# A two-layer graph network with a mixture of experts behind it: one-hots made at other times and in other pieces, bias products with all 128 rows

## The chip, the cores and the metric

The kernel runs on one NeuronCore of a Trainium2 chip. The metric is the time of one execution on the device in microseconds (us), as the median of several runs. The engines are TensorE (PE in the profile; its weight loads, which overlap its matmuls, are PEld), VectorE (DVE), ScalarE (ACT), GpSimd (POOL) and SyncE (SP), which only issues DMAs here.

## The reference

```python
x = x + gnn(layernorm(x))          # x: 6250 nodes x 256, float32
x = x + ffn(layernorm(x))

def rgcn_conv(x, src, dst, edge_type, basis, comp, root, bias):   # R = 8 relations, 4 bases
    W = einsum('rb,bde->rde', comp, basis)
    h = einsum('nd,rde->nre', x, W)
    msg = h[src, edge_type]                      # 206250 edges, sorted by dst
    seg = dst * 8 + edge_type
    mean = segment_sum(msg, seg) / maximum(count(seg), 1)
    return mean.reshape(n, 8, -1).sum(1) + x @ root + bias

h = relu(rgcn_conv(x, ..., layer 0))
h = relu(rgcn_conv(h, ..., layer 1))
gnn = take(einsum('nd,tde->nte', h, lin_w), node_type) + lin_b[node_type]   # 5 node types

# ffn: 8 experts, top 2, D = 256, H = 512
logits = xn @ Wr + br
w = softmax of the top 2 logits, spread over the 8 experts
y = sum over e of w[:, e] * (gelu(xn @ W1[e] + b1[e]) @ W2[e] + b2[e])
```

## The kernel before, in words

Nodes are taken in pairs of blocks: a block is 64 nodes, a pair 128, and there are 49 pairs. The edges are sorted by destination, so a block's edges lie in one window, cut in 18 tiles of 128 edges. For each tile GpSimd gathers 128 rows of the node table (each row three bf16 parts of 256 features) with one indirect DMA (L558) into one of 18 slots. The last tile's gather is issued only where it holds edges. A tile's edges hit at most 64 of the block's 512 (node, relation) columns. VectorE makes a one-hot of 128 x 64 for every tile, all 18 of a block in one instruction (L929): the column numbers `iota_b` compared with each edge's `rel`. TensorE multiplies the gathered rows by the one-hot into PSUM (L1251, six matmuls a tile; in layer 0 a seventh, L1247, counts the edges).

When a block's 18 tiles are summed, VectorE scales the sums by 1/count into `scaled` (`scale`, L945). In layer 0 it first makes `inv` from the counts (L938, L939); in layer 1 `inv` comes back from memory. For a pair, `mix_bases` (L911 for the first relation, L913 for the other seven) mixes the eight relations into four bases, and TensorE's `transform` (L1283) multiplies them by the bases. `h` is 0 for the even block of a pair and 1 for the odd one; `hot`, `idx`, `rel` and `inv` are double over it.

Who waits for whom: a gather waits for its slot to be free (`used[k]`, raised by TensorE every third tile); a tile's matmuls wait for the gather; a block's first tile waits for its one-hots (`hot_ready`) and for VectorE to have scaled the block before it (`sc_ready`), since both sum into the same banks; `one_hots` waits for the tables that SP loads (`idx_in`) and for the block that used the same half of `hot`. SP works through one list: the even block's tables, the even block's `inv`, behind the odd block's scale, the odd block's tables, its `inv`, the node data.

Layer 0's loop (`first_layer` on VectorE) goes, for pair p: scale the even block, one-hots of the next even block, scale the odd block, `save`, mix, one-hots of the next odd block. Layer 1's loop (`second_layer`; `dense` on TensorE and ScalarE) does three pairs at once: block work of one pair, the type-wise product and layer norm of the pair before it (`typed`, `margin`, `route`), and the eight experts of the pair before that. The order is written out by hand: on VectorE, one-hots of the next even block, root and masks, experts 0 and 1, `typed`, expert 2, scale the odd block, mix, `margin`, mix, expert 3, `route`, then mixing and experts 4, 5 and 6 in turn, one-hots of the next odd block, scale the even block, expert 7. `plain` is a memset of one column that holds a wait ahead of a branch.

Three products bring a bias in with few rows: the types' bias (L1314, `tmaskT` of 5 rows times `linb_sb`), the experts' second bias (L1410, `wfT` of 8 rows times `b2_sb`), and the router's bias (L1329, one row of ones times `br_sb`). The last is added to the logits in PSUM (L1328 gives the logits), and VectorE copies them out (L997).

Of the kernel before, what the change touches and what calls it, by code (L numbers as in the profile page):

```python
# [68 lines left out]
def build(nc, x, src, dst, etype, ntype, basis0, comp0, root0, bias0, basis1, comp1, root1, bias1,  # L69
          lin_w, lin_b, gamma, beta, Wr, br, W1, b1, W2, b2, out):  # L70
    with ExitStack() as ctx:
# [37 lines left out]
        linb_sb = sb("linb_sb", [TYPES, D], F32)  # L109
        b2_sb = sb("b2_sb", [EXPERTS, D], F32)  # L110
        br_sb = sb("br_sb", [1, EXPERTS], F32)
# [18 lines left out]
        tmaskT = sb("tmaskT", [TYPES, P], F32)  # L130
# [15 lines left out]
        wfT = sb("wfT", [EXPERTS, P], F32)  # L146
# [191 lines left out]
        def _(sp):  # L338
# [41 lines left out]
            sp.dma_start(linb_sb[:, :], lin_b).then_inc(weights_in, 16)  # L380
            sp.dma_start(b2_sb[:, :], b2).then_inc(weights_in, 16)
            sp.dma_start(br_sb[:, :], br.rearrange("(a e) -> a e", a=1)).then_inc(weights_in, 16)
# [139 lines left out]
        def _(gp):  # L522
# [17 lines left out]
            gp.iota(pid[:, :], [[0, 1]], base=0, channel_multiplier=1, allow_small_or_imprecise_dtypes=True)  # L540
            gp.memset(ident[:, :], 0.0).then_inc(s_const, 1)
# [77 lines left out]
        def _(act_):  # L619
# [79 lines left out]
            def dense(a=None, r=None, n=P):  # L699
                if r is not None:  # L700
                    gelu(r, 0)
                    gelu(r, 1)
                if a is not None:
                    relu(1, a + PAIRS, a)
                if r is not None:
                    gelu(r, 2)
                if a is not None:
                    deviation(a, 0)
                    deviation(a, 1)
                if r is not None:  # L710
                    gelu(r, 3)
                if a is not None:
                    act_.wait_ge(znT_done, START + a + 1)
                    if not isinstance(a, int) or a > 0:
                        act_.wait_ge(lg_done, a)
                    for k in range(HALVES):
                        last = sc.activation(xnext[:, k, :], T2[:, k * P:(k + 1) * P], ACT.Identity,
                                             bias=beta_sb[:, k:k + 1], scale=gamma_sb[:, k:k + 1])
                    last.then_inc(xnext_done, 1)
                if r is not None:  # L720
                    gelu(r, 4)
                if a is not None:
                    act_.wait_ge(margin_done, a + 1)
                    sc.activation(soft[:, 1:2], soft[:, 0:1], ACT.Tanh, scale=0.5).then_inc(tanh_done, 1)
                if r is not None:
                    gelu(r, 5)
                    gelu(r, 6)
                    act_.wait_ge(wfT_ps, r + 1)
                    sc.activation(wfT[:, :], T2[0:EXPERTS, 256:256 + P], ACT.Copy).then_inc(wfT_done, 1)
                    gelu(r, 7)  # L730
                if a is not None:
                    act_.wait_ge(xnext_done, a + 1)
                    sc.activation(xnT[:, :, :], xnext[:, :, :], ACT.Copy).then_inc(xnT_done, 1)
                if r is not None:
                    act_.wait_ge(y_acc, 2 * START + (r + 1) * EXPERTS)
                    act_.dma_start(out[bass.ds(r * P, n), :], o[0:n, :]).then_inc(out_done, 16)
# [9 lines left out]
        def _(dve):  # L746
# [173 lines left out]
            def one_hots(h, G):  # L920
                with dve.If(general):
                    pass
                with dve.Else():
                    one_hots_fast(h, G)

            def one_hots_fast(h, G):
                dve.wait_ge(idx_in[h], G * 48 + 48)
                summed(dve, G, h, back=2)
                v.tensor_tensor(hot[:, h, :, :], iota_b[:, :].unsqueeze(1).broadcast_to([P, TILES, COLS]),  # L929
                                rel[:, h, :].unsqueeze(2).broadcast_to([P, TILES, COLS]),  # L930
                                ALU.is_equal).then_inc(hot_ready, 1)
# [44 lines left out]
            def masks(p):  # L976
                dve.wait_ge(node_in, p * 48 + 48)
                v.tensor_scalar(tmask[:, :], iota8[:, 0:TYPES], ntcol[:, 0:1], None, ALU.is_equal)
                v.tensor_scalar(tmaskT[:, :], ntrow[:, :], pid[0:TYPES, 0:1], None,
# [15 lines left out]
            def margin(p):  # L995
                dve.wait_ge(lg_done, p + 1)
                v.tensor_copy(lg[:, :], LG).then_inc(lg_read, 1)  # L997
# [34 lines left out]
            def first_layer():  # L1032
                one_hots(0, 0)
                one_hots(1, 0)
                for h in range(2):
                    scale(0, h, 0, 0)
                    if h == 0:
                        one_hots(0, 1)
                mix_bases(0, 0)
                one_hots(1, 1)  # L1040
                base = ch.base + ch.n

                def body(p, more=True):
                    scale(0, 0, p, p)
                    if more:
                        one_hots(0, p + 1)
# [3 lines left out]
                    if more:  # L1050
                        one_hots(1, p + 1)
# [10 lines left out]
            def second_layer():  # L1062

                def body(a=None, r=None, y=None, x=None):
                    if x is not None:
                        plain(1)
                        one_hots(0, x + PAIRS)
# [21 lines left out]
                    for e, (first, last_) in ((4, (8, 16)), (5, (16, 24)), (6, (24, MIXES))):  # L1089
                        if y is not None:  # L1090
                            mix_bases(1, y + PAIRS, first, last_)
                        if r is not None:
                            expert(r, e)
                    if x is not None:
                        plain(3)
                        one_hots(1, x + PAIRS)
# [7 lines left out]
                one_hots(0, PAIRS)  # L1104
                plain(3)
                one_hots(1, PAIRS)
# [25 lines left out]
        def _(pe):  # L1132
# [190 lines left out]
            def logits(q):  # L1323
# [3 lines left out]
                for k in range(HALVES):  # L1327
                    t.matmul(LG, xnext[:, k, :], wr_sb[:, k, :], start=(k == 0), stop=False)  # L1328
                t.matmul(LG, ones_f[0:1, :], br_sb[:, :], start=False, stop=True).then_inc(lg_done, 1)  # L1329
# [156 lines left out]
```

## Time and profile before

| | |
|---|---|
| median of 3 runs | 4807.63 us (4806.77 to 4810.96) |
| the profiled execution's own time | 4807.05 us |
| its span | 4805.2 us |
| PE busy | 3782.7 us, 79% |
| PEld busy | 3282.0 us, 68% |
| DVE busy | 3014.4 us, 63% |
| ACT busy | 880.3 us, 18% |
| POOL busy | 3332.3 us, 69% |

Busy time is the time in which an engine had an instruction of its own running; waits, branches and the issuing of a DMA by SP or ACT are not in it. Matmuls are pipelined, so a busy PE is not a PE at its peak. Some 200 us of setting up (layer norm, tables) come first, then layer 0 to about 2350 us, then layer 1, and the last pairs' experts from 4700 us on. The shares of the whole span mix these stages.

### The profile page before, as it was taken

The page shows a single profiled execution, that of the slowest core. Times are in us where ns is not written, and L with a number is a line of the kernel's source. Part 1 is how long each engine was busy: PE and PEld are TensorE (multiplying, and loading weights), DVE is VectorE, ACT ScalarE, POOL GpSimd, SP SyncE. Part 2 cuts the span into 40 slices and gives each one's busy share as a digit, 9 for nine tenths or more (in the row PEclk, how much of TensorE's full clock was granted, in tenths as well). Part 3 has the DMA queues.
Part 4 walks back from the last instruction along what each step waited for, and adds up shares of the span by engine and source line. Part 5 has one row for each costly group of instructions (what it writes and reads, how often), then busy time and mean ns, then how long its engine had stood idle before and what let it go on. Part 6 is the DMA issues. An engine that isn't in the chain of part 4 may idle for free.

```text
span 4805.2 us, 119647 instructions
## 1 busy us (share of the span) xinstructions
PE 3782.7 (79%) x38119; PEld 3282.0 (68%) x38120; DVE 3014.4 (63%) x6579; ACT 880.3 (18%) x2470; POOL 3332.3 (69%) x3374
## 2 busy tenths in 40 slices
PE   1366666666666666666559999999999999999999
PEld 1255555555555555555448888888888888888888
DVE  4556656766666676666446676767666666666663
ACT  2200000000000000000003333333333333333333
POOL 0477777777777777777477777777777777676770
PEclk9555555555555555555569999999999999999999
DMA  4656655555555555555456555555555555555550
GB/s 128 194 172 183 176 158 156 158 158 157 156 158 158 155 159 157 156 157 159 115 168 168 160 160 160 157 161 156 160 159 162 157 160 161 157 161 157 162 160 21
DMA packets 344661, 749.10 MB, mean 156 GB/s; under 512 B 128323, under 2 KB 167806, under 8 KB 344430
## 3 DMA queue, kind: packets, MB, share of 16 engines
q0 software_dynamic: 215040, 662.09, 49.0%
q1 hardware_dynamic: 115510, 70.49, 5.6%
q10 hardware_dynamic: 14076, 16.04, 1.0%
q8 instruction: 23, 0.38, 0.0%
q14 instruction: 12, 0.10, 0.0%
HBM read 719.00 MB, written 29.35 MB: 156 GB/s over the span
## 4 chain that ended last, share of the span: by engine, by line
PE 43%; DVE 24%; issue 15%; DMA 9%; POOL 8%; DVEq 1%; SPq 0%; ACT 0%; POOLq 0%; ACTq 0%
DVE mixed L913 11%; POOL slot L558 8%; PE bank L1251 8%; PE bank L1338 8%; PE bank L1283 8%; PE bank L1351 8%; DMA slot<-table,idx 7%; DVE inv L939 4%; PE bank L1247 3%; DVE scaled L945 3%; PE bank L1311 2%; PE bank L1312 2%; DVE o L1024 2%; PE bank L1279 1%; DVE inv L938 1%
## 5 line engine op out<-in xcount | busy, mean ns | idle before, releaser
L558 POOL DMA_INDIRECT slot<-table,idx x3354 | 3326.6, 992 | 1308.2 <-issue 1045.0
L1251 PE MATMUL bank<-hot,slot 128*128 (+1 forms) x21168 | 1240.9, 211 | 63.2 <-DMA slot<-table,idx 54.6
L1251 PEld LDWEIGHTS bank<-hot,slot 128*128 128x128 bf16 x21168 | 994.4, 108 | 125.6 <-issue 69.2
L1247 PE MATMUL bank<-hot,ones_b 128*128 x1764 | 398.7, 226 | 744.9 <-DMA slot<-table,idx 337.8
L1247 PEld LDWEIGHTS bank<-hot,ones_b 128*128 128x128 bf16 x1764 | 180.9, 103 | 1007.1 <-issue 969.3
L1338 PE MATMUL bank<-xnT,ffn_w 128*128 128x128 f32 x6272 | 791.4, 279 | 49.2 <-DVE scaled L945 49.1
L1338 PEld LDWEIGHTS bank<-xnT,ffn_w 128*128 128x128 f32 x6272 | 740.7, 192 | 80.7 <-DVE scaled L945 58.3
L1351 PE MATMUL bank<-ffn_w,act 128*128 128x256 f32 x3136 | 761.6, 386 | 0.3 <-DVE o L1024 0.2
L1351 PEld LDWEIGHTS bank<-ffn_w,act 128*128 128x128 f32 x3136 | 565.5, 190 | 78.0 <-issue 16.9
L913 DVE SCALAR_TENSOR_TENSOR mixed<-scaled,small,mixed 128x256 f32<-128x256 f32 x1372 | 573.7, 481 | 12.2
L913 DVE SCALAR_TENSOR_TENSOR mixed<-scaled,comp_sb,mixed 128x256 f32<-128x256 f32 x1372 | 573.5, 481 | 10.5
L938 DVE TENSOR_SCALAR inv<-bank 128x512 f32<-128x512 f32 x98 | 67.5, 689 | 777.3 <-PE bank L1251 777.3
L691 ACT ACTIVATE act<-bank,small 128x128 f32<-128x128 f32 x1568 | 441.7, 373 | 542.6 <-PE bank L1338 541.5
L1283 PE MATMUL bank<-mixed,basis_sb 128*128 128x128 f32 x3136 | 472.2, 310 | 0.0
L1283 PEld LDWEIGHTS bank<-mixed,basis_sb 128*128 128x128 f32 x3136 | 451.7, 227 | 0.0
L945 DVE TENSOR_TENSOR scaled<-bank,inv 128x512 f32<-128x512 f32 x392 | 377.0, 1039 | 62.2 <-PE bank L1251 48.7
L939 DVE RECIPROCAL inv<-inv 128x512 f32<-128x512 f32 x98 | 328.6, 3353 | 3.4
L1024 DVE SCALAR_TENSOR_TENSOR o<-bank,wfull,o 128x256 f32<-128x256 f32 x343 | 164.9, 481 | 252.6 <-PE bank L1351 247.5
L929 DVE TENSOR_TENSOR hot<-iota_b,rel 128x1152 bf16<-128x1152 bf16 x196 | 265.0, 1353 | 44.4 <-issue 29.7
L665 ACT ACTIVATE hcur<-bank,small 128x128 f32<-128x128 f32 x98 | 30.6, 363 | 1118.0 <-PE bank L1283 1027.2
L691 ACT ACT_TABLE_LOAD x96 | 123.2, 1283 | 374.3 <-DVE o L1024 373.4
L988 DVE SCALAR_TENSOR_TENSOR x<-bank,tmask,x 128x256 f32<-128x256 f32 x196 | 94.9, 484 | 116.3 <-PE bank L1312 116.3
(148 smaller groups left out, 2189.0 us busy)
## 6 DMA issues: line engine op xcount, KB each, us to landing
slot<-table,idx POOLq DMA_INDIRECT x3354
inv<-inv_d SPq DMA_DIRECT2D x98, 256.0 KB, 3.7
table<-ffn_w SPq DMA_DIRECT2D x7, 1344.0 KB, 6.0
table<-parts ACTq DMA_DIRECT2D x49, 192.0 KB, 3.2
ffn_w<-in_L_ffn_W_dram SPq DMA_DIRECT2D x16, 512.0 KB
xcur<-in_x_dram SPq DMA_DIRECT2D x48, 128.0 KB
out_dram<-o ACTq DMA_DIRECT2D x48, 128.0 KB
ffn_w<-in_x_dram SPq DMA_DIRECT2D x6, 896.0 KB, 8.9
```

Of the source, the lines that this page charges most:

```text
L558: gp.indirect_dma_start(out=slot[:, k, :], out_offset=None, in_=table[layer], in_offset=bass.IndirectOffsetOnAxis(ap=idx[:, h, k:k + 1], a ...
L691: last = sc.activation(act[:, e % 2, c, :], HP[e % 2][:, c * P:(c + 1) * P], ACT.Gelu, bias=b1_sb[:, e * HCH + c:e * HCH + c + 1])
L913: ins = v.scalar_tensor_tensor(out=mixed[:, b, :, :], in0=scaled[:, :, r, :], scalar=s, in1=mixed[:, b, :, :], op0=ALU.mult, op1=ALU.add)
L929: v.tensor_tensor(hot[:, h, :, :], iota_b[:, :].unsqueeze(1).broadcast_to([P, TILES, COLS]), rel[:, h, :].unsqueeze(2).broadcast_to([P, TI ...
L939: ch.link(v.reciprocal(iv, iv))
L945: last = v.tensor_tensor(scaled[:, k, :, h * BD:(h + 1) * BD].rearrange("p r n -> p n r"), S[k][:, :].rearrange("p (n r) -> p n r", r=R), ...
L1024: v.scalar_tensor_tensor(out=o[:, :], in0=YP[e % 2][:, 0:D], scalar=wfull[:, 0, e:e + 1], in1=acc[:, :], op0=ALU.mult, op1=ALU.add).then_i ...
L1247: t.matmul(C[:, at], ones_b[:, :], oh, start=(k == 0), stop=(k == TILES - 1), skip_group_check=True)
L1251: last = t.matmul(S[f][:, at], slot[:, k, q * D + f * P:q * D + (f + 1) * P], oh, start=(k == 0 and q == 0), stop=(k == TILES - 1 and q == ...
L1283: last = t.matmul(T[:, o_ * P:(o_ + 1) * P], basis_sb[:, b, k, o_ * P:(o_ + 1) * P], mixed[:, b, k, :], start=(layer == 1 and n == 1), sto ...
L1338: last = t.matmul(HP[e % 2][:, c * P:(c + 1) * P], w1_sb[:, e, k, c * P:(c + 1) * P], xnT[:, k, :], start=(k == 0), stop=(k == HALVES - 1))
L1351: last = t.matmul(YP[e % 2][:, 0:D], act[:, e % 2, c, :], w2_sb[:, e, c, :], start=(c == 0), stop=(c == HCH - 1))
```

## The change

1. In layer 1, the one-hots of the next odd block are made behind expert 5, and no longer behind expert 6 and its bias sum.
2. In layer 0, the one-hots of a block are made in 18 instructions of one tile each (a tensor_scalar with `rel` as a scalar per row), and no longer in one tensor_tensor. Layer 1 keeps the one instruction.
3. `tmaskT`, `wfT`, `linb_sb` and `b2_sb` get 128 rows. GpSimd sets them to zero at the start; the masks, weights and biases fill the first 5 or 8 rows, and the two products run over 128 rows. SP waits for GpSimd's third constant before it loads the biases.
4. The router's bias is loaded to all 128 rows and added by VectorE as it takes the logits out of PSUM; TensorE's product for it goes.

```diff
-        linb_sb = sb("linb_sb", [TYPES, D], F32)
-        b2_sb = sb("b2_sb", [EXPERTS, D], F32)
-        br_sb = sb("br_sb", [1, EXPERTS], F32)
+        linb_sb = sb("linb_sb", [P, D], F32)
+        b2_sb = sb("b2_sb", [P, D], F32)
+        br_sb = sb("br_sb", [P, EXPERTS], F32)
...
-        tmaskT = sb("tmaskT", [TYPES, P], F32)
+        tmaskT = sb("tmaskT", [P, P], F32)
...
-        wfT = sb("wfT", [EXPERTS, P], F32)
+        wfT = sb("wfT", [P, P], F32)
...
-            sp.dma_start(linb_sb[:, :], lin_b).then_inc(weights_in, 16)
-            sp.dma_start(b2_sb[:, :], b2).then_inc(weights_in, 16)
-            sp.dma_start(br_sb[:, :], br.rearrange("(a e) -> a e", a=1)).then_inc(weights_in, 16)
+            sp.wait_ge(s_const, 3)
+            sp.dma_start(linb_sb[0:TYPES, :], lin_b).then_inc(weights_in, 16)
+            sp.dma_start(b2_sb[0:EXPERTS, :], b2).then_inc(weights_in, 16)
+            sp.dma_start(br_sb[:, :], br.partition_broadcast(P)).then_inc(weights_in, 16)
...
+            for z in (linb_sb, b2_sb, tmaskT, wfT):
+                gp.memset(z[:, :], 0.0)
...
-                    sc.activation(wfT[:, :], T2[0:EXPERTS, 256:256 + P], ACT.Copy).then_inc(wfT_done, 1)
+                    sc.activation(wfT[0:EXPERTS, :], T2[0:EXPERTS, 256:256 + P], ACT.Copy).then_inc(wfT_done, 1)
...
-            def one_hots_fast(h, G):
-                dve.wait_ge(idx_in[h], G * 48 + 48)
-                summed(dve, G, h, back=2)
-                v.tensor_tensor(hot[:, h, :, :], iota_b[:, :].unsqueeze(1).broadcast_to([P, TILES, COLS]),
-                                rel[:, h, :].unsqueeze(2).broadcast_to([P, TILES, COLS]),
-                                ALU.is_equal).then_inc(hot_ready, 1)
+                    dve.wait_ge(idx_in[h], G * 48 + 48)
+                    summed(dve, G, h, back=2)
+                    if layer == 0:
+                        for k in range(TILES):
+                            last = v.tensor_scalar(hot[:, h, k, :], iota_b[:, :], rel[:, h, k:k + 1], None,
+                                                   ALU.is_equal)
+                    else:
+                        last = v.tensor_tensor(hot[:, h, :, :],
+                                               iota_b[:, :].unsqueeze(1).broadcast_to([P, TILES, COLS]),
+                                               rel[:, h, :].unsqueeze(2).broadcast_to([P, TILES, COLS]),
+                                               ALU.is_equal)
+                    last.then_inc(hot_ready, 1)
...
-                v.tensor_scalar(tmaskT[:, :], ntrow[:, :], pid[0:TYPES, 0:1], None,
+                v.tensor_scalar(tmaskT[0:TYPES, :], ntrow[:, :], pid[0:TYPES, 0:1], None,
                                 ALU.is_equal).then_inc(mask_done, 1)
...
-                v.tensor_copy(lg[:, :], LG).then_inc(lg_read, 1)
+                v.tensor_tensor(lg[:, :], LG, br_sb[:, :], ALU.add).then_inc(lg_read, 1)
...
+                        if e == 5 and x is not None:
+                            plain(3)
+                            one_hots(1, 1, x + PAIRS)
                     if x is not None:
-                        plain(3)
-                        one_hots(1, x + PAIRS)
                         scale(1, 0, x + PAIRS, x)
...
-                    t.matmul(LG, xnext[:, k, :], wr_sb[:, k, :], start=(k == 0), stop=False)
-                t.matmul(LG, ones_f[0:1, :], br_sb[:, :], start=False, stop=True).then_inc(lg_done, 1)
+                    last = t.matmul(LG, xnext[:, k, :], wr_sb[:, k, :], start=(k == 0), stop=(k == HALVES - 1))
+                last.then_inc(lg_done, 1)
```

## Rows read from the trace of the kernel before

**Rows 1.** Stretches: busy us (x instructions) of PE, PEld, DVE, ACT, POOL; clock, DMA.

```profile
300.00:2260.00 1960.00, 1309.24 (x13372) 1055.21 (x13371) 1241.97 (x1980) 62.64 (x176) 1498.72 (x1515) 0.58 0.57 160
2360.00:4700.00 2340.00, 2209.64 (x22533) 2005.18 (x22534) 1506.28 (x4025) 721.20 (x2048) 1664.71 (x1677) 0.97 0.57 159
```

**Rows 2.** Line L558 from 300 to 2260 us: ns minimum/median/maximum, first and last start.

```profile
L558 POOL DMA_INDIRECT slot<-table,idx x1515: 942/946/1865, 299.4 to 2259.9; - x190
```

**Rows 3.** GpSimd in order of time, layer 0: start, us, instruction, idle before it.

```profile
1041.11 1.36 POOL L558 DMA_INDIRECT slot<-table,idx  x1 [0.30 <-issue]
...
1047.77 1.83 POOL L558 DMA_INDIRECT slot<-table,idx  x1 [0.31 <-issue]
...
1071.14 1.01 POOL L558 DMA_INDIRECT slot<-table,idx  x1 [0.30 <-issue]
```

**Rows 4.** VectorE in order of time, a pair of layer 0.

```profile
1040.30 1.35 DVE L929 TENSOR_TENSOR hot<-iota_b,rel 128x1152 bf16<-128x1152 bf16 x1
1041.57 0.69 DVE L938 TENSOR_SCALAR inv<-bank 128x512 f32<-128x512 f32 x1
...
1047.45 1.34 DVE L929 TENSOR_TENSOR hot<-iota_b,rel 128x1152 bf16<-128x1152 bf16 x1
1063.84 0.69 DVE L938 TENSOR_SCALAR inv<-bank 128x512 f32<-128x512 f32 x1 [15.05 <-PE bank L1251]
...
1071.25 1.27 DVE L911 TENSOR_SCALAR mixed<-scaled,small 128x256 f32<-128x256 f32 x4
...
1085.66 0.69 DVE L938 TENSOR_SCALAR inv<-bank 128x512 f32<-128x512 f32 x1
```

**Rows 5.** TensorE's matmuls in order of time: tiles 0 and 11 of an odd block, layer 0.

```profile
1047.95 0.20 PE L1247 MATMUL bank<-hot,ones_b 128*128 x1 [0.82 <-DVE scaled L945]
...
1055.79 0.23 PE L1247 MATMUL bank<-hot,ones_b 128*128 x1
```

**Rows 6.** VectorE in order of time, a period of layer 1.

```profile
3057.54 0.17 DVE L997 COPY lg<-bank 128x8 f32<-128x8 f32 x1 [0.55 <-PE bank L1329]
...
3073.06 0.42 DVE L1029 TENSOR_TENSOR o<-o,bank 128x256 f32<-128x256 f32 x1
...
3073.93 1.36 DVE L929 TENSOR_TENSOR hot<-iota_b,rel 128x1152 bf16<-128x1152 bf16 x1 [0.33 <-issue]
3075.21 1.90 DVE L945 TENSOR_TENSOR scaled<-bank,inv 128x512 f32<-128x512 f32 x2
...
3083.90 0.22 DVE L978 TENSOR_SCALAR tmask<-iota,ntcol 128x5 f32<-128x5 f32 x1
3084.03 0.47 DVE L979 TENSOR_SCALAR tmaskT<-ntrow,pid 5x128 f32<-5x128 int32 x1
...
3101.23 1.96 DVE L945 TENSOR_TENSOR scaled<-bank,inv 128x512 f32<-128x512 f32 x2 [0.22 <-DVE o L1024]
...
3104.98 0.17 DVE L997 COPY lg<-bank 128x8 f32<-128x8 f32 x1 [0.40 <-PE bank L1329]
```

**Rows 7.** TensorE's matmuls in order of time, the same period.

```profile
3077.16 2.05 PE L1338 MATMUL bank<-xnT,ffn_w 128*128 128x128 f32 x16 [1.07 <-DVE scaled L945]
...
3094.52 0.59 PE L1311 MATMUL bank<-linw_sb,hcur 128*128 128x256 f32 x2
3094.95 0.59 PE L1312 MATMUL bank<-linw_sb,hcur 128*128 128x256 f32 x2
...
3096.10 2.05 PE L1338 MATMUL bank<-xnT,ffn_w 128*128 128x128 f32 x16
...
3104.05 0.51 PE L1328 MATMUL bank<-wr_sb,xnext 128*128 128x8 f32 x4
3104.49 0.38 PE L1329 MATMUL bank<-br_sb,ones_f 1*128 1x8 f32 x2
```

**Rows 8.** GpSimd in order of time, layer 1: its one long wait in a period.

```profile
3060.76 0.94 POOL L558 DMA_INDIRECT slot<-table,idx  x1 [3.47 <-PE bank L1251]
```

More of the change, by code:

```diff
@@ L918, in mix_bases, with one_hots @@
                     ins.then_inc(mixed_ready, 1)
-            def one_hots(h, G):
+            def one_hots(layer, h, G):
                 with dve.If(general):
@@ L923, in one_hots @@
                 with dve.Else():
-                    one_hots_fast(h, G)
-            def one_hots_fast(h, G):
-                dve.wait_ge(idx_in[h], G * 48 + 48)
-                summed(dve, G, h, back=2)
-                v.tensor_tensor(hot[:, h, :, :], iota_b[:, :].unsqueeze(1).broadcast_to([P, TILES, COLS]),
-                                rel[:, h, :].unsqueeze(2).broadcast_to([P, TILES, COLS]),
-                                ALU.is_equal).then_inc(hot_ready, 1)
+                    dve.wait_ge(idx_in[h], G * 48 + 48)
[10 more added lines that the diff above has]
+                    last.then_inc(hot_ready, 1)
             def scale(layer, h, G, p):
@@ L1032, in first_layer @@
             def first_layer():
-                one_hots(0, 0)
-                one_hots(1, 0)
+                one_hots(0, 0, 0)
+                one_hots(0, 1, 0)
                 for h in range(2):
@@ L1037, in first_layer @@
                     if h == 0:
-                        one_hots(0, 1)
+                        one_hots(0, 0, 1)
                 mix_bases(0, 0)
-                one_hots(1, 1)
+                one_hots(0, 1, 1)
                 base = ch.base + ch.n
@@ L1045, in body @@
                     if more:
-                        one_hots(0, p + 1)
+                        one_hots(0, 0, p + 1)
                     scale(0, 1, p, p)
@@ L1050, in body @@
                     if more:
-                        one_hots(1, p + 1)
+                        one_hots(0, 1, p + 1)
                 per = 4 + (R - 1)
@@ L1066, in body @@
                         plain(1)
-                        one_hots(0, x + PAIRS)
+                        one_hots(1, 0, x + PAIRS)
                     if a is not None:
@@ L1103, in second_layer @@
                 plain(1)
-                one_hots(0, PAIRS)
+                one_hots(1, 0, PAIRS)
                 plain(3)
-                one_hots(1, PAIRS)
+                one_hots(1, 1, PAIRS)
                 scale(1, 0, PAIRS, 0)
```

## The prediction, made before the changed kernel was run

> **What bounds the kernel now.** I read first the table of stretches [rows 1]: a piece of layer 0's loop, then layer 1's loop. In layer 0 no engine looks full: GpSimd is busy 1498.72 of 1960 us, VectorE 1242, TensorE 1309 at a granted clock of 0.58. In layer 1 TensorE is busy 2209.64 of 2340 us at 0.97. Two stages, two limits.
>
> For layer 0 the next view is GpSimd's one line, the gathers [rows 2]: 1515 in 1960 us, median 946 ns, mean 1498.72/1515 = 989 ns, each with 0.30 us of issue ahead of it [rows 3]. 1498.7 + 1515 x 0.30 = 1953 us: the stretch is filled by gathers and their gaps, and layer 0 lasts as long as its gathers. Mean over median is 43 ns x 1515 = 65 us in 1960, or 1.5 us of each pair of blocks; a pair takes 1085.66 - 1041.57 = 44.09 us [rows 4]. What makes some of them long is seen by holding GpSimd's order of time [rows 3] against VectorE's [rows 4]. The gather at 1041.11 took 1.36 us instead of 0.95; the one-hots of a whole block (L929) ran from 1040.30 to 1041.65. The gather at 1047.77 took 1.83; the other one-hots ran from 1047.45 to 1048.79. Both gathers ended some 0.8 us after the one-hots: a gather that begins inside that instruction stands until it is over, and then takes what it has left. That is 0.41 + 0.88 = 1.3 us of each pair, nearly all of the 1.5.
>
> For layer 1 I read both engines in order of time [rows 6, 7]. The period is 3104.98 - 3057.54 = 47.44 us, in two halves. From the logits' copy (3057.54) to the end of the even block's `scaled` (3077.11), 19.6 us, VectorE goes through margin, mixing, experts 3 to 6, one-hots and scale and is late: TensorE stood 1.07 us before 3077.16 for it. From there to the end of the logits (3104.87), 27.7 us, TensorE sets the time. What TensorE saves in its half counts; what it saves in VectorE's half doesn't.
>
> **Layer 0's one-hots, tile by tile.** Removed per pair: two instructions of 1.27 us (1040.30 to 1041.57 [rows 4]), and with them 1.3 us of GpSimd's time. Added: 36 compares of 64 columns with one scalar per row. The trace has none of that size; the nearest rows bound it. `tmask` (L978), 5 columns and a scalar per row, is followed by L979 after 0.13 us [rows 6]: the lower bound. L911, 256 columns, takes 1.27 us for four, the last 0.35 at most, so (1.27 - 0.35)/3 = 0.31 each [rows 4]: the upper bound. 64 columns are a quarter of the way, so I take 0.13 + 0.18/4 = 0.175 us. A set of 18 is 3.15 us (bounds 2.3 and 5.6), 1.9 more than now.
>
> What does such a train do to a gather? The nearest row is the gather at 1071.14, which meets L911's four from 1071.25 on and takes 1.01 us: 0.06 over [rows 3, 4]. It doesn't stand until a train is over, but for a part of one instruction. A set of 3.15 us meets 2.5 gathers (one each 1.25 us), two sets 5: 0.3 us a pair (bounds nothing, and 0.13 each, a whole compare: 0.65). GpSimd saves 1.3 - 0.3 = 1.0 us a pair; in 47 pairs **-47 us**, if GpSimd stays the limit.
>
> Does it? The ring behind it: odd block's `inv` over mixing and odd one-hots to the even block's `inv` (1063.84 to 1085.66, 21.8 us); that `inv` to TensorE's first tile of the odd block (1041.57 to 1047.95, 6.4); its 18 tiles at TensorE's own pace (1047.95 to 1055.79 for 11, 0.71 each, 12.8) [rows 4, 5]. That is 41.0 us against 44.1, so TensorE still catches up with the gathers. The longer set lies in this ring: 42.9 against 44.1 - 1.0 = 43.1. The cover is used up to 0.2 us. The even one-hots (1047.45) lie before 15 us of VectorE's idle time and cost nothing.
>
> The Trainium skill (SBUF — State Buffer, "Who interferes with whom") says that VectorE and GpSimd share a port pair as an exclusive lock, and that a tensor_scalar in a two-port mode takes it; the gathers that end right behind L929 agree with blocking, and L911's row shows only 0.06 us of it. The Trainium skill (VectorE: DVE Perf Modes, "The TRN2 errata") speaks against many small tiles: 58 + FD/Accel cycles each, an estimate of 77 ns a compare, 1.4 us a set; no row is that fast.
>
> **Router's bias.** TensorE's two L1329 go, so `lg` can start when L1328 ends, 3104.05 + 0.51 = 3104.56, not 3104.87 [rows 7]: **-0.31 us**, at the seam of the halves. The add in place of the 0.17 us copy has one input more; I take 0 and bound it at 0.02.
>
> **128 rows for the bias products.** L1312 starts 0.43 us after L1311 (3094.52 to 3094.95), two matmuls of 256 columns. L1338 could then start 0.86 us after L1312, with the 5-row L1314 between; it starts at 3096.10, 1.15 after it [rows 7]. So a visit to 5 rows costs 0.29 us; **-0.29** in TensorE's half. Below it may be nothing (given back by the layer norm's chain on VectorE and ScalarE), above 0.4. L1410 (8 rows) lies in VectorE's half: nothing. The Trainium skill (TensorE: Matmul & The Clock Gate, "LDWEIGHTS") has a load of 32 rows take as long as one of 128; by that alone padding would bring nothing, and the gap in the row speaks against it.
>
> **Odd one-hots two experts ahead.** They stay in VectorE's unbroken half, so their 1.27 us and the 0.45 in front of them (3073.48 to 3073.93, memset and branch) are paid earlier, not saved. What is hidden changes: `scaled` at 3075.21 started before the one-hots had ended, its semaphore checks covered. Directly behind an expert's sum it starts 0.22 us late (3101.23) [rows 6], and here there is one check more. **+0.25 us** a period; bounds 0 and 0.35. Queued behind them are mixing's last quarter, expert 6 and the b2 sum, 1.7 us later; only the next transform, 6 us on, needs those. SP loads their `rel` behind the odd `scaled` of 3101.23, some 14 us before they want it. A gather may stand 0.9 us for them, but GpSimd waits 3.47 us for used slots each period [rows 8].
>
> Layer 1: -0.31 - 0.29 + 0.25 = -0.35 us, x 48 = **-17 us**. The four memsets and SP's wait on them lie at the start, where VectorE waits for the edges: 0. The last two bodies have no blocks: about -1.
>
> **Sum.** The profiled execution took 4807.05 us (span 4805.2), the median is 4807.63, 0.6 above. 4807.6 - 47 - 17 - 1 = 4742.6; I say **4742**.
>
> **Rivals.** (a) VectorE's ring takes over in layer 0. For it: 0.2 us of cover. It begins at 43.1 - 41.0 = 2.1 us more a set, 0.187 us a compare. At 0.22 the ring is 43.7, layer 0 gives 0.4 x 47 = 19, the time is 4771; at 0.31 the ring is 45.3, 1.2 us longer than a pair now, and it is 4846. Against it: four times fewer columns than L911. Chance 0.17, 0.03 of it beyond 0.24.
> (b) A set holds GpSimd out to its end, as one instruction does now. It decides from the first gather that starts in a set: it would stand 3.15 us less its offset, some 2.4 on average, twice a pair, instead of 1.3: +3.5 us, x 47 = +164, 4953. Against it: the gather of 1.01 us at L911's four. It needs compares that follow each other without a gap for GpSimd. Chance 0.05. A lock as the Trainium skill has it ends with each instruction.
> (c) The padded rows bring nothing: 4742 + 14 = 4756. Chance 0.10.
> (d) The moved one-hots cost nothing: 4742 - 12 = 4730. Chance 0.15.
> The forecast itself: 0.53.
>
> **Numbers.** The range goes from all of 1.3 us saved together with (d), 4742 - 14 - 12 = 4716, to the middle of (a) with (c), 4785; outside are (b) and the far end of (a). This kernel's measurement tells about 0.2% (9.6 us) from no change. Faster 0.90, same 0.03 (between the two ends of (a)), slower 0.07.
>
> **What would show it.** After: layer 0's pair at 43.1 us; no gather of 1.36 or 1.83 beside the one-hots; sets of 2.3 to 3.3 us; GpSimd's gap still 0.30 at every gather. Layer 1: a period of 47.1 us, L1338 0.43 behind the bias product, `scaled` 0.2 to 0.35 behind the b2 sum. Wrong would be: gathers that wait for TensorE's L1251 in layer 0 (a), or gathers of 2 us and more (b).

## The result, and the profile after

| | before | after |
|---|---|---|
| median, us | 4807.2 (4804.32 to 4810.96, 4 runs) | 4725.92 (4724.51 to 4728.75, 4 runs) |
| the profiled execution's own time | 4807.05 | 4726.16 |
| its span | 4805.2 | 4724.1 |

The ratio is 0.9831, with a 95% interval of 0.9814 to 0.9848: 81 us less, where 65 were forecast.

Where the 81 us come from is read off the first and last gather of each layer. The view is the gathers' source line, over the whole of layer 0 and the whole of layer 1: ns minimum/median/maximum, then first and last start. First the kernel before:

```profile
L558 POOL DMA_INDIRECT slot<-table,idx x1677: 942/946/2149, 173.2 to 2344.7; - x187
...
L558 POOL DMA_INDIRECT slot<-table,idx x1677: 940/946/1898, 2389.9 to 4694.2; - x187
```

And the changed kernel:

```profile
L561 POOL DMA_INDIRECT slot<-table,idx x1677: 942/946/1152, 173.2 to 2282.3; - x187
...
L561 POOL DMA_INDIRECT slot<-table,idx x1677: 940/946/1978, 2326.7 to 4615.8; - x187
```

Both reach the first gather at 173.2 us. Layer 0's gathers take 2109.1 us instead of 2171.5 (-62.4), the step between the layers 44.4 instead of 45.2 (-0.8), layer 1's gathers 2289.1 instead of 2304.3 (-15.2), and what follows the last gather 4724.1 - 4615.8 = 108.3 instead of 111.0 (-2.7). Forecast were -47, 0, -17 and -1. The longest gather of layer 0 fell from 2149 to 1152 ns, while layer 1 still has its long ones.

Layer 0's stretch of the changed kernel, as in [rows 1]:

```profile
300.00:2260.00 1960.00, 1357.56 (x13754) 1089.45 (x13754) 1411.20 (x3585) 64.87 (x182) 1485.43 (x1559) 0.58 0.58 165
```

In the same 1960 us of layer 0 there are 1559 gathers instead of 1515, in less busy time: 1485.43/1559 = 953 ns on average instead of 989. 1485.4 + 1559 x 0.30 = 1953 us: gathers and their gaps fill the stretch as before. GpSimd is still the limit, and the granted clock is the same 0.58. None of the 1576 gathers that start between 300 us and the layer's end has more than 0.35 us of idle time ahead of it, so none waited for TensorE.

VectorE in order of time, a pair of layer 0, beside [rows 4]:

```profile
1036.61 0.69 DVE L945 TENSOR_SCALAR inv<-bank 128x512 f32<-128x512 f32 x1 [10.96 <-PE bank L1259]
...
1045.33 11.92 DVE L916 SCALAR_TENSOR_TENSOR mixed<-scaled,small,mixed 128x256 f32<-128x256 f32 x28
1057.17 3.03 DVE L931 TENSOR_SCALAR hot<-iota_b,rel 128x64 bf16<-128x64 bf16 x18
1059.87 0.68 DVE L945 TENSOR_SCALAR inv<-bank 128x512 f32<-128x512 f32 x1
...
1065.74 2.77 DVE L931 TENSOR_SCALAR hot<-iota_b,rel 128x64 bf16<-128x64 bf16 x18
1079.33 0.69 DVE L945 TENSOR_SCALAR inv<-bank 128x512 f32<-128x512 f32 x1 [10.82 <-PE bank L1259]
```

The pair is 1079.33 - 1036.61 = 42.72 us here, 42.79 as the median of all. A set takes 1059.87 - 1057.17 = 2.70 us, 0.15 a compare. GpSimd beside it, as in [rows 3]:

```profile
1049.05 1.01 POOL L561 DMA_INDIRECT slot<-table,idx  x1 [0.30 <-issue]
...
1057.99 0.95 POOL L561 DMA_INDIRECT slot<-table,idx  x1 [0.30 <-issue]
1059.24 0.96 POOL L561 DMA_INDIRECT slot<-table,idx  x1 [0.30 <-issue]
...
1066.75 0.95 POOL L561 DMA_INDIRECT slot<-table,idx  x1 [0.30 <-issue]
1068.00 0.95 POOL L561 DMA_INDIRECT slot<-table,idx  x1 [0.30 <-issue]
```

The four gathers that begin in the two sets take 0.95 and 0.96 us. Over the whole of layer 0 from 300 us on, 182 gathers begin inside a compare and take 950 ns on average, 979 at most: next to nothing. The gathers of 1.01 us lie beside the mixing, which is the same in both kernels.

Layer 1, VectorE in order of time, beside [rows 6]:

```profile
2989.63 0.17 DVE L1004 TENSOR_TENSOR lg<-bank,br_sb 128x8 f32<-128x8 f32 x1 [0.16 <-PE bank L1336]
...
3001.74 1.36 DVE L934 TENSOR_TENSOR hot<-iota_b,rel 128x1152 bf16<-128x1152 bf16 x1 [0.33 <-issue]
...
3006.82 0.42 DVE L1036 TENSOR_TENSOR o<-o,bank 128x256 f32<-128x256 f32 x1
3007.57 1.89 DVE L952 TENSOR_TENSOR scaled<-bank,inv 128x512 f32<-128x512 f32 x2 [0.33 <-DVE o L1036]
```

TensorE in the same period, beside [rows 7]:

```profile
2989.01 0.51 PE L1336 MATMUL bank<-wr_sb,xnext 128*128 128x8 f32 x4
2989.37 2.03 PE L1346 MATMUL bank<-xnT,ffn_w 128*128 128x128 f32 x16
...
3009.52 2.05 PE L1346 MATMUL bank<-xnT,ffn_w 128*128 128x128 f32 x16 [1.75 <-DVE scaled L952]
3011.41 0.69 PE L1259 MATMUL bank<-hot,slot 128*128 128x64 bf16 x18
3011.93 3.82 PE L1291 MATMUL bank<-mixed,basis_sb 128*128 128x128 f32 x32
3015.58 1.89 PE L1359 MATMUL bank<-ffn_w,act 128*128 128x256 f32 x8
...
3027.30 0.59 PE L1320 MATMUL bank<-linw_sb,hcur 128*128 128x256 f32 x2
3027.74 0.65 PE L1322 MATMUL bank<-linb_sb,tmaskT 128*128 128x256 f32 x2
3028.22 1.95 PE L1346 MATMUL bank<-xnT,ffn_w 128*128 128x128 f32 x16
```

The period's median is 47.11 us instead of 47.43. From `lg` to the end of the even `scaled` it is 3009.46 - 2989.63 = 19.83 us (before 3077.11 - 3057.54 = 19.57): +0.26. The rest is 27.28 instead of 27.87: -0.6. TensorE's wait for `scaled` grew from 1.07 to 1.75 us, since TensorE arrives 0.42 us earlier and VectorE 0.26 later: what was saved of TensorE's work in VectorE's half turned into that wait (e4 and e5 below show the parts).

### The profile page after: what moved, and what is told of

The parts are those of the page before. It is cut to its first block, busy times and chain, and to the rows that moved or that the text cites. A ratio compares the mean times of both kernels' runs of the same rounds, so it can differ in the third digit from the quotient of the medians.

```text
span 4724.1 us, 121121 instructions
## 1 busy us (share of the span) xinstructions
PE 3743.5 (79%) x38021; PEld 3276.7 (69%) x38022; DVE 3155.1 (67%) x8245; ACT 880.1 (19%) x2470; POOL 3283.6 (70%) x3378
## 4 chain that ended last, share of the span: by engine, by line
PE 38%; DVE 36%; issue 15%; POOL 5%; DMA 4%; DVEq 1%; ACT 0%; SPq 0%; POOLq 0%; ACTq 0%
DVE mixed L916 17%; PE bank L1259 9%; PE bank L1346 8%; PE bank L1359 8%; DVE inv L946 6%; POOL slot L561 5%; PE bank L1291 4%; PE bank L1255 3%; DVE scaled L952 3%; PE bank L1319 2%; DMA slot<-table,idx 2%; PE bank L1320 2%; DVE hot L931 2%; DVE o L1031 1%; DVE mixed L914 1%
## 5 line engine op out<-in xcount | busy, mean ns | idle before, releaser
L561 POOL DMA_INDIRECT slot<-table,idx x3354 | 3277.0, 977 | 1279.6 <-issue 1043.7
L1259 PE MATMUL bank<-hot,slot 128*128 (+1 forms) x21168 | 1254.9, 213 | 63.1 <-DMA slot<-table,idx 54.3
L1346 PE MATMUL bank<-xnT,ffn_w 128*128 128x128 f32 x6272 | 786.1, 279 | 80.6 <-DVE scaled L952 80.6
L1346 PEld LDWEIGHTS bank<-xnT,ffn_w 128*128 128x128 f32 x6272 | 745.9, 193 | 97.3 <-DVE scaled L952 89.4
L931 DVE TENSOR_SCALAR hot<-iota_b,rel 128x64 bf16<-128x64 bf16 x1764 | 280.7, 260 | 6.4 <-DMA off<-off_d 6.4
```

What stands on the lines that cost most here:

```text
L561: gp.indirect_dma_start(out=slot[:, k, :], out_offset=None, in_=table[layer], in_offset=bass.IndirectOffsetOnAxis(ap=idx[:, h, k:k + 1], a ...
L931: last = v.tensor_scalar(hot[:, h, k, :], iota_b[:, :], rel[:, h, k:k + 1], None, ALU.is_equal)
L1259: last = t.matmul(S[f][:, at], slot[:, k, q * D + f * P:q * D + (f + 1) * P], oh, start=(k == 0 and q == 0), stop=(k == TILES - 1 and q == ...
L1346: last = t.matmul(HP[e % 2][:, c * P:(c + 1) * P], w1_sb[:, e, k, c * P:(c + 1) * P], xnT[:, k, :], start=(k == 0), stop=(k == HALVES - 1))
```

## The experiments

"Pair" is the median distance of the even blocks' `inv` in layer 0, "period" that of `lg` in layer 1. Every time stands beside runs of the kernel before on the same chip. "..." in a diff stands for lines left out. For the first four that kernel took 4811.54 us (15 runs).

**e1, the one-hots by tiles in layer 0, nothing else.**

```diff
...
+                    for k in range(TILES):
+                        last = v.tensor_scalar(hot[:, h, k, :], iota_b[:, :], rel[:, h, k:k + 1], None,
+                                               ALU.is_equal)
+                    last.then_inc(hot_ready, 1)
...
```

> The kernel before with layer 0's one-hots made tile by tile and nothing else. Theory (a gather that begins inside the whole-block one-hots stands until they end; short compares don't hold it): layer 0's pair goes from 44.09 to 42.8 us as in the changed kernel, gathers in layer 0 average 0.95 us, layer 1's period stays 47.43; 4807 - 62 = 4745 us. The sum as forecast (0.06 us for each gather met) would give 4760. Rival (layer 0's gain comes from somewhere else in the change): 4800 to 4807.

Measured: 4748.07 us, ratio 0.9867 (0.9850 to 0.9883), 63.5 us less. Pair 42.85, period 47.43 as before, a gather of layer 0 956 ns on average. So the whole gain of layer 0 is this part's.

**e2, the changed kernel with the odd one-hots back behind expert 6.**

```diff
-                        if e == 5 and x is not None:
-                            plain(3)
-                            one_hots(1, 1, x + PAIRS)
                     if x is not None:
+                        plain(3)
+                        one_hots(1, 1, x + PAIRS)
```

> The changed kernel with the odd one-hots of layer 1 back behind expert 6 and its bias sum. Theory (the move only uncovers the semaphore checks ahead of the even scale, 0.26 us of VectorE's unbroken half): period of layer 1 47.11 - 0.26 = 46.85 us, 4726 - 12 = 4714 us. Rival (being early helps: experts or TensorE wait less): period 47.11 or more, 4726 us or more.

Measured: 4718.31 us, ratio 0.9805 (0.9789 to 0.9822), period 46.85. The changed kernel's period is 0.25 us longer, 48 x 0.25 = 12 us. By the medians it is 7.6 us slower, but the two stood beside different runs of the kernel before; by their ratios (0.9831 and 0.9805) it is 12 us too. The move is a loss.

**e3, the kernel before with that move alone** (the opposite diff).

> The kernel before with only the odd one-hots of layer 1 made behind expert 5. Theory: period of layer 1 47.43 + 0.26 = 47.69 us, 4807 + 12 = 4819 us. Rival (the move is free): 4807; (the move helps) under 4800.

Measured: 4823.36 us, ratio 1.0027 (1.0018 to 1.0037), period 47.71: +0.28. In this kernel the even `scaled` starts behind 0.33 us of idle time, as it does at 3007.57 above.

**e4, 128 rows for the two bias products, nothing else** (the change's third part).

> The kernel before with only the two bias products over 128 rows (zeroed rows, SP's wait). Theory (5 rows cost TensorE 0.29 us more than 128 in its own half of the period, 8 rows cost nothing because TensorE waits there): period 47.43 - 0.30 = 47.13 us, 4807 - 15 = 4792 us. Rival (the number of rows doesn't matter): 47.43, 4807 us. Rival (given back by the layer norm's chain): gaps on TensorE gone, but y of expert 2 found waiting for the norm, 47.4.

Measured: 4796.28 us, ratio 0.9969 (0.9957 to 0.9982), period 47.14: -0.29; pair 44.12. TensorE's wait for `scaled`:

```profile
3077.39 2.05 PE L1341 MATMUL bank<-xnT,ffn_w 128*128 128x128 f32 x16 [1.35 <-DVE scaled L948]
```

It is 1.36 us as the median of the periods instead of 1.07, while VectorE's half, from `lg` to the end of the even `scaled`, stays at 19.55 us. So the 128 rows of the experts' product save TensorE some 0.29 us in VectorE's half, and all of it comes back as waiting; the period's gain is that of the types' product.

**e5, the router's bias by VectorE, nothing else** (the fourth part). Here and for e6 to e8 the kernel before took 4808.18 us (10 runs).

> The kernel before with only the router's bias taken from TensorE and added by VectorE. Theory (the logits' end lies at the seam of the two halves): period of layer 1 47.43 - 0.31 = 47.12 us, 15 us less than the kernel before beside it. Rival (TensorE has slack, VectorE's mixing ends as late): 47.43, the same time.

Measured: 4793.39 us, ratio 0.9970 (0.9958 to 0.9981), period 47.15: -0.28. TensorE's wait for `scaled` is 1.16 us. The parts add up: 47.43 - 0.29 - 0.28 = 46.86, and e2 has 46.85.

**e6, e2 with TensorE's wait for `scaled` put behind the up products of the first two experts, no longer between them.** `open_block` holds the waits for `sc_ready` and `hot_ready`, `ups(e)` are an expert's first products, and `more` runs the block's first three tiles.

```diff
                 ups(0)
+                ups(1)
                 more = open_block(y, 1)
-                ups(1, RUN)
+                more(RUN)
```

> The kernel of e2_no_move with one change on TensorE: in layer 1 the wait for the even block's scale stands behind the up products of expert 1, which don't need it, and no longer ahead of them. Theory (TensorE stands some 1.5 us a period at that wait, 19.6 us of VectorE's half being the longer way): the wait is covered by 1.8 us of matmuls, the period goes from 46.85 to 45.4 us, 70 us less than e2_no_move, 4648 us. Rival (the wait isn't what sets the period; it is slack that comes back as another wait, of GpSimd's gathers above all, 34.2 x 1.25 = 42.8 us and 1.5 of long ones): 46.5 to 46.9 us, less than 20 us gained.

Measured: 4671.92 us, ratio 0.9720 (0.9703 to 0.9736). Period 45.88: 0.97 less than e2's, not the 1.5 expected. TensorE's wait for `scaled`, 1.44 us in e2, is gone, but the block's first tiles suffer. TensorE in order of time:

```profile
2947.18 3.73 PE L1345 MATMUL bank<-xnT,ffn_w 128*128 128x128 f32 x32
2950.75 0.34 PE L1258 MATMUL bank<-hot,slot 128*128 128x64 bf16 x6
2951.30 0.79 PE L1258 MATMUL bank<-hot,slot 128*128 128x64 bf16 x12 [0.22 <-issue]
2952.10 2.13 PE L1290 MATMUL bank<-mixed,basis_sb 128*128 128x128 f32 x17
```

VectorE's `scaled` in the same view:

```profile
2948.63 1.94 DVE L952 TENSOR_TENSOR scaled<-bank,inv 128x512 f32<-128x512 f32 x2
```

Three tiles are 0.52 us elsewhere (3011.41 to 3011.93 in the changed kernel); here they take 2952.10 - 2950.75 = 1.35. `scaled` ends at 2950.57, just before them. My reading: TensorE's sequencer stood at the wait until then, behind the queued products, and only afterwards prepared the tiles' addresses. e12 tests where the wait stands; what the sequencer does is in no view.

**e7, layer 0's one-hots in three instructions of six tiles**, in the old form (on the kernel before).

```diff
...
+                    for k in range(0, TILES, 6):
+                        last = v.tensor_tensor(hot[:, h, k:k + 6, :],
+                                               iota_b[:, :].unsqueeze(1).broadcast_to([P, 6, COLS]),
+                                               rel[:, h, k:k + 6].unsqueeze(2).broadcast_to([P, 6, COLS]),
+                                               ALU.is_equal)
...
```

> The kernel before with layer 0's one-hots in three instructions of six tiles, in the same form (tensor_tensor, two inputs from SBUF) as the one. Theory (a gather that begins inside an instruction of this form stands until that instruction is over, whatever follows): each piece is 0.53 us long, a gather loses at most that and 0.25 on average over those that begin in a set; layer 0's gathers average 0.955 to 0.975 us, the pair 43.0 to 43.5 us, 30 to 50 us less than before. Rival (the form itself is at fault, and a set holds gathers for its whole 1.6 us): gathers over 0.99 us, pair 44.1 or more.

Measured: 4776.95 us, ratio 0.9934 (0.9918 to 0.9951): half of e1's gain. Pair 43.41, gathers 972 ns. The total came as expected, but the rows show something more. The pieces' own line (ns minimum/median/maximum):

```profile
L931 DVE TENSOR_TENSOR hot<-iota_b,rel x270: 523/551/564, 328.7 to 2259.7; 128x384 bf16<-128x384 bf16 x135
```

In order of time, the two sets of a pair, then the two gathers that meet them:

```profile
1069.18 1.49 DVE L931 TENSOR_TENSOR hot<-iota_b,rel 128x384 bf16<-128x384 bf16 x3
1076.48 1.46 DVE L931 TENSOR_TENSOR hot<-iota_b,rel 128x384 bf16<-128x384 bf16 x3
...
1069.99 1.50 POOL L558 DMA_INDIRECT slot<-table,idx  x1 [0.30 <-issue]
...
1076.80 1.04 POOL L558 DMA_INDIRECT slot<-table,idx  x1 [0.30 <-issue]
```

Pieces of 0.55 us start (1.49 - 0.55)/2 = 0.47 apart, so the second set's first piece ends at 1077.03; the gather of 1076.80 ended at 1077.84, 0.81 later, as the gathers of [rows 3] do behind L929. It stood for one piece. The gather of 1069.99 began in the second piece, which ended at 1070.20; it ended at 1071.49, 0.82 after the third piece (1070.67). It stood through two pieces. So cutting the instruction does not always let a gather in between: the next piece can take over. It goes by where in a piece the gather begins. Of the 91 gathers that begin in a piece, the 45 that begin 0.17 to 0.33 us after its start stood for that piece alone; the 45 that begin 0.34 to 0.36 us after the start of a second piece stood for the third as well; one that begins 0.02 us into a set stood through all three (2.28 us).

Is it the instruction's length or its form (two tensors from SBUF instead of one tensor and a scalar per row)? The trace of the kernel before says more on this than the experiment. VectorE, then GpSimd, in layer 0:

```profile
1064.57 3.35 DVE L939 RECIPROCAL inv<-inv 128x512 f32<-128x512 f32 x1
1070.91 0.43 DVE L960 TENSOR_TENSOR parts<-rest,parts 128x256 bf16<-128x256 f32 x1 [0.48 <-ACT parts L674]
...
1064.90 0.94 POOL L558 DMA_INDIRECT slot<-table,idx  x1 [0.30 <-issue]
1066.15 0.94 POOL L558 DMA_INDIRECT slot<-table,idx  x1 [0.30 <-issue]
```

The reciprocal, with one tensor as input, is 3.35 us long and holds neither gather. Of the 1580 gathers of layer 0 from 300 us on, 932 overlap no VectorE instruction with two tensors from SBUF, 326 of them the reciprocal: none takes more than 955 ns. Of the 70.8 us over the median that layer 0's gathers take, 70.5 lie in the other 648. So length alone holds no gather here. One tensor as input is no guarantee either: in layer 1, 49 gathers beside float32 tensor_scalars of 256 columns (L911, L969) take up to 1.08 us. What a whole block's one-hots would do as one instruction with a scalar input was not run.

**e8, e2 with layer 1's odd one-hots by tiles as well.**

```diff
-                    if layer == 0:
+                    if layer == 0 or h == 1:
```

> The kernel of e2_no_move with the odd one-hots of layer 1 tile by tile too. Theory (they lie in VectorE's unbroken half, which is the longer way): a set takes 2.6 us instead of 1.27, the period goes from 46.85 to 48.2 us, 65 us more than e2_no_move. Rival (GpSimd's long gathers matter in layer 1 as in layer 0): the period falls under 46.85.

Measured: 4866.67 us, ratio 1.0125 (1.0102 to 1.0148), period 49.80. The sign is right; the loss against e2, 2.95 us a period and 148 us in all, is more than double what was expected. TensorE in order of time in one period:

```profile
3093.90 3.79 PE L1345 MATMUL bank<-xnT,ffn_w 128*128 128x128 f32 x16 [2.88 <-DVE scaled L952]
3097.48 1.17 PE L1258 MATMUL bank<-hot,slot 128*128 128x64 bf16 x18
3098.46 4.51 PE L1290 MATMUL bank<-mixed,basis_sb 128*128 128x128 f32 x32
3102.80 1.89 PE L1358 MATMUL bank<-ffn_w,act 128*128 128x256 f32 x8
```

The windows ahead of and over these rows (columns as in [rows 1]):

```profile
3076.00:3091.00 15.00, 15.00 (x170) 13.76 (x168) 14.25 (x45) 2.71 (x10) 11.65 (x12) 1.00 0.48 136
3093.90:3102.80 8.90, 8.90 (x66) 8.84 (x67) 1.88 (x4) 3.56 (x9) 6.66 (x6) 0.66 0.59 171
```

The longer set makes TensorE's stand 2.88 us instead of e2's 1.44. Then the same three groups take 3102.80 - 3093.90 = 8.90 us where the changed kernel needs 6.06 (3009.52 to 3015.58): 2.84 more, at a granted clock of 0.66 on average, so that part of them ran at the lower level, 1.2 GHz instead of 2.4. The periods of this run bear it out. The stand is there in each of 46 periods, 2.86 to 3.14 us long, but the clock of the 8.9 us behind it is not the same: 1.00 in 7 of them, with periods of 48.2 to 48.6 us; 0.81 to 0.84 in 20, with 49.5 to 50.1; 0.65 to 0.68 in 19, with 51.0 to 51.3. The first is e2's 46.85 and the 1.43 us of the longer set, which is what was expected; the last is that and the 2.84 us. What decides between the three these runs don't show.

**e9, e10, e11, all three beside a kernel before of 6062.01 us (6029.54 to 6099.13, 15 runs).** e9 is e6 with the opening put behind `transform` as well (the diff below, against e2); e10 is e6's edit on the changed kernel, with the move; e11 is the kernel before with 128 rows for `wfT` and `b2_sb` only.

```diff
                 ups(0)
-                more = open_block(y, 1)
-                ups(1, RUN)
+                ups(1)
                 if a is not None:
                     transform(1, a + PAIRS, a)
+                more = open_block(y, 1)
+                more(RUN)
```

> e6_late_open with the wait one step later still, behind the transform too, and the odd block's first three tiles with it. Theory (in e6_late_open TensorE has no idle time to speak of, but its sequencer stands at the wait until 2950.6 and then loads the block's registers in the open, 1.35 us for three tiles that take 0.52 elsewhere; VectorE's half is still the longer way by a hair): behind the transform the wait is long over, the period goes from 45.88 to 45.1-45.3 us, all of it TensorE's work, 30 us less than e6_late_open, 4640 us. Rival (the tiles' cost is the switch from float32 to bf16 or the gathers' pace, 44.4 us): 45.8 to 45.9.

> The changed kernel, so with the odd one-hots two experts ahead, and e6_late_open's later wait. Theory (VectorE's half still decides when the wait ends, and the move lengthens it by 0.26 us): period 45.88 + 0.26 = 46.14 us. Rival (TensorE is full and VectorE has room): 45.88 us.

> The kernel before with only the experts' bias product over 128 rows. Theory (it lies in VectorE's half, where TensorE waits 1.07 us a period afterwards; all of e4_rows_only's gain is the types' bias): period 47.43 us, and TensorE's wait for the even scale grows from 1.07 to 1.4 us; the same time. Rival (both products pay): period 47.3.

Measured: e9 6149.43 us, ratio 1.0126 (1.0086 to 1.0166), period 64.18, pair 55.21. e10 6116.23, ratio 1.0083 (1.0058 to 1.0109), 63.19 and 55.16. e11 6077.63, ratio 1.0014 (0.9990 to 1.0038), 63.02 and 53.99. On this chip the kernel before is 26% longer, and e9's kernel 33% longer than in e12 below, so none of the three questions was answered here. What differs is seen in e11, TensorE in order of time inside a tile of layer 0, and GpSimd 44 us later:

```profile
1004.43 0.21 PE L1254 MATMUL bank<-hot,slot 128*128 x1 [1.17 <-issue]
1005.15 0.39 PE L1254 MATMUL bank<-hot,slot 128*128 x4 [0.51 <-issue]
...
1047.72 0.95 POOL L561 DMA_INDIRECT slot<-table,idx  x1 [5.95 <-PE bank L1254]
```

TensorE stands 0.5 and 1.2 us between matmuls of one tile, waiting for nothing that the profile shows, and GpSimd waits for TensorE to free slots. The gathers themselves are as ever (993 ns on average in e11, 956 in e9). So GpSimd no longer sets layer 0's time. With the longer sets the pair is 1.2 us longer by the medians (55.2 against 54.0), and layer 0 from first to last gather 30 us longer (2701 and 2700 against 2670), or 0.6 us a pair, instead of 1.3 shorter. That is the sign of rival (a), the ring of VectorE and TensorE, on a chip where TensorE's instructions come late; that the sets cost it there is argued, since no run on that chip has them alone. Why the instructions come late stays open.

**e12, the kernel of e9 once more.** The kernel before took 4809.92 us (4806.15 to 4810.68, 7 runs) beside it.

> The kernel of e9 again: e6 with TensorE's opening of the odd block moved once more, behind the transform of the last tile's neighbour, so that TensorE reaches it only when VectorE has ended scaled. Theory (what e6 still lost, 0.5 us a period, is TensorE's sequencer standing at the wait until scaled ends and only then loading the registers of the block's first tiles): where the kernel before takes about 4808 us beside it, layer 1's period is 45.1 to 45.6 instead of e6's 45.88 and the time 4635 to 4660 us, pair of layer 0 42.8. Rival (TensorE's later opening only moves the same work behind the later tile and makes VectorE's first compare late): the period 45.8 to 46.3 and the time 4670 to 4695. If the kernel before takes about 6060 beside it, as in e9, neither can be told and the ratio is 1.00 to 1.02 again.

Measured: 4640.35 us (4639.93 to 4640.95, 4 runs), ratio 0.9649 (0.9632 to 0.9665), period 45.05, pair 42.83. It beats the kernel before by 170 us and the changed kernel, which ran at another time, by some 86. The period is just under the 45.1 to 45.6 expected. TensorE in order of time around the place:

```profile
2942.14 3.73 PE L1345 MATMUL bank<-xnT,ffn_w 128*128 128x128 f32 x32
2945.71 3.74 PE L1290 MATMUL bank<-mixed,basis_sb 128*128 128x128 f32 x32
2949.28 0.69 PE L1258 MATMUL bank<-hot,slot 128*128 128x64 bf16 x18
2949.80 1.97 PE L1358 MATMUL bank<-ffn_w,act 128*128 128x256 f32 x8
```

There is no idle time left, and the three tiles take 0.52 us again. Against e6 this is 0.84 us a period: exactly what the slow tiles cost there (1.35 - 0.52 = 0.83). So the tiles were slow because of where the wait stood: e9's rival (the switch from float32 to bf16, which is here too) and e12's (the opening only moves) fall. It fits the reading of e6, without showing the sequencer itself.

The numbers also say what a stand costs beside the wait. The same work in e2:

```profile
3053.92 1.95 PE L1345 MATMUL bank<-xnT,ffn_w 128*128 128x128 f32 x16
3057.32 2.05 PE L1345 MATMUL bank<-xnT,ffn_w 128*128 128x128 f32 x16 [1.46 <-DVE scaled L952]
...
3063.39 1.89 PE L1358 MATMUL bank<-ffn_w,act 128*128 128x256 f32 x8
```

From the first L1345 to L1358 TensorE needs 3063.39 - 3053.92 = 9.47 us here and 2949.80 - 2942.14 = 7.66 in e12: 1.81 less, of which the wait is 1.46. So 0.35 us more goes with the stand. That also explains e6, where the slow tiles gave part of it back: 1.81 - 0.83 = 0.98, and 0.97 was measured.

## Why the prediction was right, and where its sizes were off

**What bounds layer 0** was right: after the change, gathers and gaps still fill the stretch, and e1's gain of 63.5 us comes with the gathers' mean alone (956 ns).

**Layer 0's term was too small: -62.4 us, not -47.** Its step was "five gathers met, 0.06 us each: 0.3 us a pair" given back. The term measured is next to nothing: the 182 gathers that begin in a compare take 950 ns on average, so all of the 1.3 us is kept. The price came from a misread row. The gather of 1071.14 begins inside L960, a tensor_tensor that runs from 1070.91 to 1071.34 (shown under e7), and not in L911's train, which starts at 1071.25; so it is no price for scalar compares. In layer 0 of the kernel before, the 55 gathers that begin inside L911 take 949 ns at most (in layer 1 some take more). A smaller part is the count: gathers run over 49 pairs, 62.4/49 = 1.27 us each; I used 47. The lower end of the range already had "all of 1.3 us saved".

**The compare was put at 0.175 us and takes 0.15,** a set 2.70 us instead of 3.15. That weakens rival (a): the cover, put at 0.2 us, is 42.8 - (41.0 + 1.4) = 0.4 us by the same sum, even with the shorter pair. The Trainium skill (VectorE: DVE Perf Modes, "The TRN2 errata") would have had 77 ns by its formula, and says itself that the formula comes out short of its own measurement; the rows show twice the 77.

**Rival (a)** fell here: no gather of layer 0 waited for TensorE. On the chip of e9 to e11 gathers did wait for TensorE, but in e11, without the longer sets, as well.

**Rival (b)** fell for the compares. Its mechanism is real for instructions of the old form: in e7 gathers stood through two and three pieces. The Trainium skill (SBUF — State Buffer, "Who interferes with whom") has a tensor_scalar in a two-port mode block GpSimd for its whole length. It also has a tensor_tensor with both inputs in SBUF contend with GpSimd's reads, and infers that it does not stop descriptor generation. The rows here speak against that inference: 1.36 and 1.83 us for a gather's issue beside the tensor_tensor [rows 3, 4]. On tensor_scalars they are split: the float32 ones of layer 1 hold a gather for up to 0.14 us, the compares of 64 columns hold it for 5 ns on average. Whether the compares run in a two-port mode no row shows.

**Layer 1's three terms** were right in place and size. Router's bias -0.31: e5 gives -0.28. Five rows to 128 -0.29: e4 gives -0.29, and L1346 starts 0.48 us behind the padded product, 0.92 behind L1320 instead of 1.15 [rows 7], which is 0.23 of it. The experts' product was put at nothing, and e4's wait of 1.36 us shows that. The move +0.25: e2 gives +0.25, e3 +0.28, with `scaled` 0.33 us behind the sum. So rivals (c) and (d) fell. The time measured, 4725.9, lies nearer to (d)'s 4730 than to the forecast, but not by its mechanism: layer 0 gave the difference, and the move cost what was said. The period fell by 0.32 us (47.43 to 47.11), over 48 periods 15.4, against the 15.2 found; forecast was 17. The end gave -2.7 us, not -1: the last bodies keep both bias savings on the path. What follows the last gather is 109.5 us in e4 and 110.3 in e5 instead of 111.0, 2.2 of the 2.7.

The four pieces add up: -62.4 - 0.8 - 15.2 - 2.7 = -81.1, the difference of the spans. Every part of the gain has a place; the 0.8 us between the layers has no cause shown.

## What to carry to other kernels

An engine that issues gathers can be slowed by what another engine runs at the instant a gather starts; look for the gathers that are over the median and hold their start times against VectorE's long instructions. A price for such an encounter holds only for the operation inside which the gather begins: the forecast's 0.06 us were put down to a train of scalars, and the gather had begun in the tensor_tensor ahead of it. Before moving work earlier in an unbroken stretch of the limiting engine, count what its old place was hiding (here the semaphore checks of `scaled`); and put a wait in TensorE's stream only where its event is already past and some work is still queued ahead of it (e6 against e12: some 30 us).

## What the runs showed of the hardware that was not expected

- With a stand of TensorE of 2.86 to 3.14 us in each period (e8), the granted clock over the next 8.9 us was 0.65 to 0.68 in 19 of 46 periods, which cost up to 2.84 us each, 0.81 to 0.84 in 20, and 1.00 in 7; with 1.75 us (after) and 1.44 us (e2) it stayed at 1.00.
- Back-to-back tensor_tensor instructions of 0.55 us let a gather in between them when it had begun up to 0.33 us after a piece's start, and not at 0.34 to 0.36 us (e7).
- A reciprocal of 3.35 us holds no gather (326 of them, 951 ns at most), where a tensor_tensor of 1.35 us holds one for up to 0.9 us.
- On one chip TensorE's instructions came with gaps of 0.5 to 1.2 us without a cause in the trace; there the kernel took 6062 us instead of 4808, and the very kernel that is 3.5% faster elsewhere (e12) was 1.3% slower (e9).
